# Overflow tiles of a top-6 mixture of experts on eight cores: taken out by GpSimd, found by halving a bit word, signalled by column halves

## The reference, cut to what matters

```python
probs = softmax(tokens @ router_w.T + router_b)
top_p, top_i = top_k(probs, 6)            # of 16 experts
gate[token, top_i] = top_p / sum(top_p)
out = sum over e of (x @ expert_w[e]) * gate[:, e]   # each 1024x1024
x = layernorm(x + out)
```

## Time and profile before

| | us |
|---|---|
| median of 3 runs | 1737.99 (1735.62 to 1738.44) |
| profiled execution, time | 1736.6 |
| its span, slowest core (0) | 1735.1 |
| its span, core with no overflow (5) | 1679.0 |
| TensorE busy | 1585.0 (91%) |
| ScalarE busy | 1307.4 (75%) |
| VectorE busy | 728.3 (42%) |
| GpSimd busy | 72.9 (4%) |

### The profile page before, as it was taken

The page is one execution under the profiler, slowest core; times in us unless marked ns, Lnnn a source line. Parts: engine busy times, 40 slices in busy tenths (PEclk is TensorE's granted clock), DMA queues, the critical chain, the costliest instruction groups (busy, mean ns, idle before and its releaser), DMA issues.

```text
span 1735.1 us, 55148 instructions; the slowest of 8 cores (1679.0 to 1735.1 us)
## 1 busy us (share of the span) xinstructions
PE 1585.0 (91%) x23176; PEld 987.5 (57%) x23176; DVE 728.3 (42%) x1722; ACT 1307.4 (75%) x1626; POOL 72.9 (4%) x55
## 2 busy tenths in 40 slices
PE   6999999999999999999977779999959999969996
PEld 3566556555665555655645445555636666636663
DVE  3132222222222222222227777666625666636587
ACT  2799999999999999999999866565525555525453
POOL 1000000000000000000000000000000000000056
PEclk9999999999999999999998889999979999989998
DMA  9920010010100100100050041026104133104012
GB/s 148 246 58 2 2 21 2 2 21 2 20 2 2 20 2 2 21 2 2 2 99 2 2 80 20 2 51 117 33 1 99 23 78 68 32 1 99 3 75 122
DMA packets 9877, 68.95 MB, mean 40 GB/s; under 512 B 1232, under 2 KB 1264, under 8 KB 6544
## 3 DMA queue, kind: packets, MB, share of 16 engines
q0 software_dynamic: 5008, 48.46, 15.6%
q1 hardware_dynamic: 4608, 16.78, 2.6%
HBM read 105.11 MB, written 8.39 MB: 65 GB/s over the span
## 4 chain that ended last, share of the span: by engine, by line
PE 81%; issue 6%; DVE 6%; ACT 3%; DVEq 2%; DMA 1%; ACTq 0%; POOL 0%; another core or an unknown queue 0%; PEldq 0%; POOLq 0%
PE s_PS L657 26%; PE s_PS L332 14%; PE s_PS L360 14%; PE s_PS L230 9%; PE s_PS L670 6%; PE s_PS L254 6%; PE s_PS L645 4%; ACT s_PR L341 3%; DVEq L171 2%; DMA s_XT<-xs 1%; DVE s_X1B L455 1%; DVE s_ST L408 1%; DVE s_KV L269 0%; DVE s_ACC L396 0%; PE s_PS L630 0%
## 5 line engine op out<-in xcount | busy, mean ns | idle before, releaser
L341 ACT ACTIVATE s_PR<-s_PS 128x1024 bf16<-128x1024 f32 x1024 | 947.9, 1204 | 42.5 <-PE s_PS L332 40.0
L332 PE MATMUL s_PS<-s_KV 64*128 64x256 bf16 x4096 | 352.8, 275 | 46.3 <-ACT s_PR L341 36.9
L729 ACT ACTIVATE s_PR<-s_PS,s_GS 128x512 bf16<-128x512 f32 x256 | 175.0, 686 | 260.4 <-PE s_PS L657 149.2
L360 PEld LDWEIGHTS s_PS<-s_KV,s_PR 128*128 128x128 bf16 x8192 | 285.0, 98 | 111.3 <-issue 111.3
L360 PE MATMUL s_PS<-s_KV,s_PR 128*128 128x65 bf16 x8192 | 347.0, 195 | 0.8 <-issue 0.8
L733 DVE SCALAR_TENSOR_TENSOR s_PR<-s_PS,s_GS,s_PR 128x512 bf16<-128x512 f32 x256 | 190.8, 749 | 228.5 <-ACT s_PR L729 220.4
L332 PEld LDWEIGHTS s_PS<-s_KV 64*128 64x128 bf16 x4096 | 142.5, 94 | 242.3 <-issue 197.1
L657 PE MATMUL s_PS<-s_KV,s_WP 128*64 128x512 bf16 x2080 | 241.2, 384 | 7.5 <-DVEq L852 3.0
L657 PE MATMUL s_PS<-s_XT,s_WP 128*64 128x512 bf16 x2080 | 242.2, 386 | 5.7 <-DVEq L852 3.0
L230 PE MATMUL s_PS<-s_XT,s_WP 128*128 128x512 bf16 x768 | 209.0, 382 | 21.4 <-DMA s_XT<-xs 15.1
L242 DVE CAST s_KV<-s_PS 128x512 bf16<-128x512 f32 x96 | 66.3, 691 | 336.6 <-PE s_PS L230 307.5
(11 more groups left out here) (93 smaller groups left out, 687.8 us busy)
## 6 DMA issues: line engine op xcount, KB each, us to landing
s_XT<-ew POOLq DMA_DIRECT2D x8, 2048.0 KB, 18.0
s_KV<-ew POOLq DMA_DIRECT2D x8, 2048.0 KB, 18.4
s_XT<-xs POOLq DMA_DIRECT2D x8, 1024.0 KB, 35.8
s_ACC<-xtm SPq DMA_DIRECT2D x16, 512.0 KB, 17.8
y<-s_ACC SPq DMA_DIRECT2D x16, 512.0 KB, 2.6
s_WP<-wp POOLq DMA_DIRECT2D x7, 768.0 KB, 7.0
s_WP<-wp POOLq DMA_DIRECT2D x1, 512.0 KB, 14.2
s_WP<-wp POOLq DMA_DIRECT2D x1, 256.0 KB, 5.8
```

What stands on the lines that cost most here:

```text
L332: return t.matmul(PS[:, o:o + 256], kt_buf(c)[rows, (kc + k) * 128:(kc + k + 1) * 128], q_buf(c)[rows, qb * 256:(qb + 1) * 256], start=Tru ...
L341: act[n] = S.tick(lambda s: s.activation(PR[:, (n % RING) * 1024:(n % RING + 1) * 1024], PS[:, i * 1024:(i + 1) * 1024], AF.Exp, bias=-3.0 ...
L360: return t.matmul(PS[:, o:o + 65], PR[:, p:p + 128], v_buf(c)[:, v0:v0 + 65], start=(kc + k == 0 and h == 0 and q == 0), stop=(kc + k == N ...
L729: hi_tok[(u, jh)] = S.tick(lambda s, h=h, b=b: s.activation(hi(u)[:, h], bank(b), AF.Copy, bias=0.0, scale=GS[:, u % 4:u % 4 + 1]))
```

## The change

1. GpSimd takes the overflow tile out (rows, gates, and the slot matrix as two comparisons of 64 columns instead of one of 128) and signals `oG`. It takes the next one when TensorE has signalled `oC`, behind the copy of the gathered tokens.
2. GpSimd and VectorE find the tile by halving: test the eight bits of each half of the word, then four, two, one. VectorE's body for a tile now begins with the wait for the gathered tokens. Its drain ahead of the search is gone.
3. TensorE gathers first and turns after. Its waits ahead of a spill, one for each token before, are now the highest value for each semaphore.
4. The two column halves of the product, of the scaling, of the low part and of the putting back are signalled one by one.
5. ScalarE copies the gathered tokens first and the turned matrix after. At the head of a round, before it waits, it does a copy of one element.
6. TensorE and ScalarE no longer wait at the end of a round for VectorE's additions. TensorE's wait for `oP` is at the head of a round. Behind each spill VectorE's list has a new drain with a signal (`added`), which joins the tokens of the two banks that the additions read.

```diff
-    many_reg, tile_reg = {}, []
+    V.do(lambda v: v.sem_inc(oP, 1))
+    V.do(lambda v: v.sem_inc(oA, 1))
+    many_reg, tile_reg = {}, {}
...
-        weights = [e_tok[2 * p], e_tok[2 * p + 1]]
-        banks_free = [tok for b in range(8) for tok in free[b]]
+        latest = {}
+        for sem, v in ([tok for b in range(8) for tok in free[b]] + [e_tok[2 * p], e_tok[2 * p + 1]]):
+            latest[id(sem)] = (sem, max(v, latest.get(id(sem), (sem, 0))[1]))
+        ready = list(latest.values())
...
-        for line in (T, V, S):
+        for line in (T, V, S, G):
             line.wait(flag_tok[0])
...
+        def tiles(e, work):
...
+            e.reg_load(word, FLG[0:1, NPE + p:NPE + p + 1])
+
+            def among(t0, t1):
+                e.reg_alu(part, word, (1 << t1) - (1 << t0), ALU.bitwise_and)
+                with e.If_ne(part, 0):
+                    if t1 - t0 == 1:
+                        work(e, t0)
+                    else:
+                        among(t0, (t0 + t1) // 2)
+                        among((t0 + t1) // 2, t1)
+
+            among(0, NT // 2)
+            among(NT // 2, NT)
...
+        def take_tile(e, t):
+            e.tensor_copy(OX, x1b(t))
+            e.tensor_copy(OG3, G3[:, (t * NE + 2 * p) * 3:(t * NE + 2 * p + 2) * 3])
+            for i in range(2):
+                col = t * NE + 2 * p + i
+                ins = e.tensor_scalar(OPUT[:, i * SLOTS:(i + 1) * SLOTS], CI[:, SLOTS:2 * SLOTS],
+                                      RK[:, col:col + 1], None, ALU.is_equal)
+            ins.then_inc(oG, 1)
+            e.wait_ge(oC, 1)
+            e.sem_clear(oC)
...
                 with e.Fori(0, n):
-                    e.wait_ge(oV, 1)
-                    for mm in turn_mms(OG3, OPUT) + gather_mms(OX, OPUT):
+                    e.wait_ge(oP, 1)
+                    e.sem_clear(oP)
+                    e.wait_ge(oG, 1)
+                    e.sem_clear(oG)
+                    for mm in gather_mms(OX, OPUT) + turn_mms(OG3, OPUT):
                         ins = mm(e)
                     ins.then_inc(oT, 1)
                     e.wait_ge(oS, 1)
-                    for mm in expert_mms(p, 0, YB[0], OXS) + expert_mms(p, 1, YB[1], OXS):
-                        ins = mm(e)
-                    ins.then_inc(oT, 1)
-                    e.wait_ge(oV, 3)
-                    for mm in back_mms(0, OPT, h0, l0) + back_mms(1, OPT, h0, l0):
-                        ins = mm(e)
-                    ins.then_inc(oT, 1)
-                    e.wait_ge(oV, 4)
+                    e.sem_inc(oC, 1)
+                    for jh in range(2):
+                        for mm in expert_mms(p, jh, YB[jh], OXS):
+                            ins = mm(e)
+                        ins.then_inc(oT, 1)
+                    for jh in range(2):
+                        e.wait_ge(oV, 2 + jh)
+                        for mm in back_mms(jh, OPT, h0, l0):
+                            ins = mm(e)
+                        ins.then_inc(oT, 1)
                     e.sem_inc(oE, 1)
-                    e.wait_ge(oP, 1)
-                    e.sem_clear(oP)
...
         def one_tile(e, t):
-            e.tensor_copy(OX, x1b(t))
-            e.tensor_copy(OG3, G3[:, (t * NE + 2 * p) * 3:(t * NE + 2 * p + 2) * 3])
-            put_op(e, OPUT, RK[:, t * NE + 2 * p: t * NE + 2 * p + 2], SLOTS).then_inc(oV, 1)
             e.wait_ge(oS, 1)
             e.reduce_sum(OGS[:, :], PS[:, MB * 512 + 128: MB * 512 + 131],
                          axis=AX.X).then_inc(oV, 1)
-            e.wait_ge(oS, 2)
             for jh in range(2):
+                e.wait_ge(oS, 2 + jh)
                 h = slice(jh * 512, (jh + 1) * 512)
-                ins = e.scalar_tensor_tensor(l0[:, h], bank(YB[jh]), OGS[:, :], h0[:, h],
-                                             ALU.mult, ALU.subtract)
-            ins.then_inc(oV, 1)
-            e.wait_ge(oT, 3)
+                e.scalar_tensor_tensor(l0[:, h], bank(YB[jh]), OGS[:, :], h0[:, h],
+                                       ALU.mult, ALU.subtract).then_inc(oV, 1)
             for jh in range(2):
+                e.wait_ge(oT, 4 + jh)
                 a = acc(t, jh * 512, (jh + 1) * 512)
-                ins = e.tensor_tensor(a, bank(OB2[jh]), a, ALU.add)
-            ins.then_inc(oV, 1)
+                e.tensor_tensor(a, bank(OB2[jh]), a, ALU.add)
+            e.drain()
             e.wait_ge(oE, 2)
...
                 with e.Fori(0, n):
-                    e.wait_ge(oT, 1)
-                    e.activation(OPT, bank(MB, 128), AF.Copy, bias=0.0, scale=1.0)
-                    e.activation(OXS, PS[:, GB * 512: GB * 512 + 1024], AF.Copy, bias=0.0,
-                                 scale=1.0).then_inc(oS, 1)
-                    e.wait_ge(oT, 2)
-                    e.wait_ge(oV, 2)
...
-                    e.wait_ge(oV, 4)
-                    e.sem_inc(oE, 1)
+                    e.activation(LG[0:1, 0:1], EX[0:1, 0:1], AF.Copy, bias=0.0, scale=1.0)
                     e.wait_ge(oA, 1)
                     e.sem_clear(oA)
+                    e.wait_ge(oT, 1)
+                    e.activation(OXS, PS[:, GB * 512: GB * 512 + 1024], AF.Copy, bias=0.0, scale=1.0)
+                    e.activation(OPT, bank(MB, 128), AF.Copy, bias=0.0, scale=1.0).then_inc(oS, 1)
+                    e.wait_ge(oV, 1)
+                    for jh in range(2):
+                        e.wait_ge(oT, 2 + jh)
+                        h = slice(jh * 512, (jh + 1) * 512)
+                        e.activation(h0[:, h], bank(YB[jh]), AF.Copy, bias=0.0,
+                                     scale=OGS[:, :]).then_inc(oS, 1)
+                    e.sem_inc(oE, 1)
...
+        added = V.tick(lambda v: v.drain())
+        for b in OB2:
+            free[b] = free[b] + [added]
```

More of the change, by code:

```diff
@@ L775, in flags @@
         flag_tok.append(V.tick(lambda v: v.tensor_copy(FLG[:, :], EX[0:1, 0:2 * NPE])))
-    oT, oV, oS, oE, oP, oA = (mksem(n) for n in ("oT", "oV", "oS", "oE", "oP", "oA"))
-    many_reg, tile_reg = {}, []
+    oT, oV, oS, oG, oC, oE, oP, oA = (
+        mksem(n) for n in ("oT", "oV", "oS", "oG", "oC", "oE", "oP", "oA"))
+    V.do(lambda v: v.sem_inc(oP, 1))
+    V.do(lambda v: v.sem_inc(oA, 1))
+    many_reg, tile_reg = {}, {}
     def spill(p, u):
         h0, l0 = hi(u + 1), lo(u + 1)
-        weights = [e_tok[2 * p], e_tok[2 * p + 1]]
-        banks_free = [tok for b in range(8) for tok in free[b]]
+        latest = {}
+        for sem, v in ([tok for b in range(8) for tok in free[b]] + [e_tok[2 * p], e_tok[2 * p + 1]]):
+            latest[id(sem)] = (sem, max(v, latest.get(id(sem), (sem, 0))[1]))
+        ready = list(latest.values())
         back = sc_tok[(u - 1, 1)]
-        for line in (T, V, S):
+        for line in (T, V, S, G):
             line.wait(flag_tok[0])
@@ L794, in many, with gpsimd @@
             return many_reg[id(e)]
+        def tiles(e, work):
+            if id(e) not in tile_reg:
+                k = len(tile_reg)
+                tile_reg[id(e)] = (e.alloc_register(f"tiles{k}"), e.alloc_register(f"tile{k}"))
+            word, part = tile_reg[id(e)]
+            e.reg_load(word, FLG[0:1, NPE + p:NPE + p + 1])
[9 more added lines that the diff above has]
+            among(NT // 2, NT)
+        def gpsimd(e):
+            n = many(e)
+            with e.If_ne(n, 0):
+                tiles(e, take_tile)
+        def take_tile(e, t):
[8 more added lines that the diff above has]
+            e.sem_clear(oC)
         def tensor(e):
@@ L798, in tensor @@
             with e.If_ne(n, 0):
-                for sem, v in banks_free + weights:
+                for sem, v in ready:
                     e.wait_ge(sem, v)
                 with e.Fori(0, n):
-                    e.wait_ge(oV, 1)
-                    for mm in turn_mms(OG3, OPUT) + gather_mms(OX, OPUT):
+                    e.wait_ge(oP, 1)
[3 more added lines that the diff above has]
+                    for mm in gather_mms(OX, OPUT) + turn_mms(OG3, OPUT):
                         ins = mm(e)
@@ L821, in vector @@
             with e.If_ne(n, 0):
-                e.drain()
-                if not tile_reg:
-                    tile_reg.extend([e.alloc_register("tiles"), e.alloc_register("tile")])
-                e.reg_load(tile_reg[0], FLG[0:1, NPE + p:NPE + p + 1])
-                for t in range(NT):
-                    e.reg_alu(tile_reg[1], tile_reg[0], 1 << t, ALU.bitwise_and)
-                    with e.If_ne(tile_reg[1], 0):
-                        one_tile(e, t)
+                tiles(e, one_tile)
         def one_tile(e, t):
-            e.tensor_copy(OX, x1b(t))
-            e.tensor_copy(OG3, G3[:, (t * NE + 2 * p) * 3:(t * NE + 2 * p + 2) * 3])
-            put_op(e, OPUT, RK[:, t * NE + 2 * p: t * NE + 2 * p + 2], SLOTS).then_inc(oV, 1)
             e.wait_ge(oS, 1)
@@ L859, in scalar @@
                 with e.Fori(0, n):
-                    e.wait_ge(oT, 1)
```

(16 more changed lines are left out.)

## The result

The changed kernel takes 0.9885 of the time before (interval 0.9866 to 0.9904), that is about 1718 us against a median of 1738.22 for the kernel before beside it; measured again the ratio is 0.9874 (0.9858 to 0.9889). Its four runs gave 1718.75, 1716.91, 1800.35 and 1836.83 us; in the last two the cores of one die ran at a granted clock of 0.87 to 0.93, so the ratio leaves them out. The profiled execution is the one of 1718.75. So the direction was right, the gain is 20 us where 30 were forecast, and the time lies about 2 us above the top of the range.

A forecast was written before the change was run, and what follows sets the result against it. It took the slowest core to be bound by TensorE plus two spills: 1681.6 us without them plus 2 x 12.4 gave a span of 1706.4, and with 1.5 above the span 1707.9, say 1707.5; range 1702 to 1716.

The forecast's parts named there:

- The base: Span of the slowest core without its spills, taken from core 4 as 1681.6 us.
- The bank wait of 1.7: Ahead of a spill, TensorE waits 1.7 us until VectorE's additions free the last bank.
- ScalarE's 1.4: Between gather and product, ScalarE's copies with hand-overs take 1.4 us, the table load hidden under the wait.
- the second half's tail of 1.6: Behind the product, only one half's scaling, low part and hand-overs remain: 1.6 us.
- The head of the round: Some eight waits and clears on TensorE as a spill begins: 0.5 us, between 0.14 and 0.78.
- Gather and turn: TensorE's gather and turning matmuls in a spill: 0.5 us, or 1.1 at the low clock.
- The product: The spill's product on TensorE: 4.9 us, the middle between 3.5 at full clock and 6.2 at the low one.
- Ends of pairs without overflow: New token and GpSimd's test at all seven pair ends cost TensorE 0, at most 0.2 us each.
- Behind the spill, 0.8 us: TensorE's next unit after a spill loses 0.8 us to slow clock or VectorE's remaining work, between 0 and 2.5.
- slower: the ends of empty pairs: Rival: late `added` costs TensorE 0 to 1.2 us at seven pair ends, 1716 us at 1.2; chance 0.03.
- The clock stays low: Rival: TensorE's clock stays low through the whole spill, 3.9 us more each, 1715 us; chance 0.13.
- VectorE's search is late: Rival: all eight search tests are long, VectorE ready 4.8 us late per spill, 1717 us; chance 0.08.

The follow-up runs named there:

- e1: Changed kernel without VectorE's drain and token behind each spill; TensorE waits for oP from the spill's body instead: 0.983 of the kernel before, two-spill mean 659.2 us against 665.3.
- e4: Changed kernel with 12 unread filler matmuls ahead of the gather and 6 ahead of the product: 0.9854 of the kernel before, two-spill mean 661.5 us.
- e2: Changed kernel with TensorE's bank wait split, the gather waiting only for banks that gather and product write: 0.9836 of the kernel before, two-spill mean 660.5 us.
- e8: Changed kernel with VectorE's body written once in a loop over tiles, only the two additions unrolled: 0.9831 of the kernel before, two-spill mean 661.0 us.

## Why the prediction was right and wrong

**Right.** The base: core 0 without its spills comes to 1682.6 us here (first gather at 1020.6, 634.4 of core 5, and 27.7 from the last gather to the end), 1.0 above the 1681.6 used. GpSimd has the tile in time: its copy begins at 1211.0, 64 us ahead of TensorE's stop, and takes 1040 ns, not 2.0:

```profile
L828 POOL COPY s_WP<-s_XT x2: 1036/1040/1044, 1211.0 to 1451.6; 128x1024 bf16<-128x1024 bf16 x2
```

The bank wait of 1.7, ScalarE's 1.4 (measured 1.5), the second half's tail of 1.6 (1.8), the putting back of 0.5 (0.6), the way out of 0.5 (0.2) and the hidden table load held. So did the direction, and the clock that falls and comes back during the product. Not so core 2: it did not come out below all cores with two spills (1708.7 against 1708.3 of core 1).

**Off in size, inside the spill: 2.0 us each.** The head of the round took 1.19 (1276.70 to 1277.89) where 0.5 was put: I knew two bounds, 0.14 and 0.78, from steps with one wait, and the head has several one behind the other. Gather and turn took 1.20, the term for the low clock, where 0.5 was taken because TensorE was to be idle for only 2.2 us; it was idle for 2.89. The product took 5.26 for 4.9. I had expected the clock to be up through the product in some spills; the trace shows 5.0 to 6.4 from the product's start to the putting back for all twelve tiles. The two spills of core 0 come to 13.5 and 13.7 for 11.6 each; the forecast was 4.0 too little.

**The step that failed: "Ends of pairs without overflow ... I take 0, at the most 0.2 each", and with it "Behind the spill, 0.8 us".** Both rest on VectorE's long step of 1.1 to 1.2. Core 0 pays 34.5 - 27.2 = 7.3 us outside its two spills, where 1.6 was forecast. The waits of TensorE on core 0 in the expert part:

```profile
PE s_PS L670 <- DVEq L912: 6.7, 4, 2.7
```

Counted by how late each unit starts behind the one before, against the same place on core 5, the 7.3 are 2.2 behind the second spill, 1.2 and 1.1 at two pairs without overflow, 2.1 at the last pair, where core 5 waits too but less, and 0.7 scattered. The argument from the earlier trace rows, that the old jump had ended by 1382.36, looked at when VectorE had to be back, not at how long its jump was, and left out that a drain behind the jump is now awaited by TensorE. "Behind the spill" had VectorE done 4 to 5 us after the putting back; behind core 0's second spill it took 6.2 (1537.31 to the drain at 1543.51), 3.09 of them one jump. Measured from test to drain, the way over sixteen bodies is 2.7 to 3.2 us at 48 of 53 places and 4.2 to 4.3 at the other five, two of them core 0's.

The rival "slower: the ends of empty pairs" had the right place and mechanism; its size was about 1 us at two of core 0's pairs and 2 at the last, far from the 4.9 for each that it needed to turn the sign.

The kernel before had the same long jump, and its trace shows it. This is core 5, without a tile, at its last two pairs, in the chain in order of time; L821 is the test for no overflow, L793 the first record of the next pair's code:

```profile
1582.70 0.06 DVEq L821
...
1586.41 0.31 DVEq L793
...
1586.75 0.06 DVEq L821
...
1589.93 0.02 DVEq L61
```

From test to next record are 3.7 and 3.2 us. At the first of these places the eight cores show 3.4 to 3.8; at the second, the five cores without a spill there show 3.1 to 3.5, and ScalarE's scaling, which VectorE needs next, had ended about 1.5 us or more before VectorE came back. So it was the jump that took the time. At nearly all other pair ends of before, among them, the next record is a wait that ends with ScalarE's scaling, and only tells that the jump took no more than 3.4 to 4.2 us. Where it can be seen the jump was no shorter before the change; what the change added is a drain behind it for which TensorE waits.

e1 is the proof: with the drain gone, core 0 got 10.8 us back, of which 7.7 lie at these four places, 1.7 in two shorter spills, and 1.4 are spread over the rest.

**Two rivals came true in part.** "The clock stays low": the gather ran at the low clock as the rival says, the put-back (0.62) and the next unit (3.64) did not, and the product was low for 3.3 of its 5.3 us. Against a product at full clock e4 puts the price at 1.6 on core 0; the rival has 2.7 and the forecast's own term 1.4. "VectorE's search is late": not on core 0, where VectorE waits for ScalarE, but on cores 1 and 6, which did not set the time. Core 1:

```profile
1605.57 5.00 PE L657 MATMUL s_PS<-s_KV,s_WP 128*64 128x512 bf16 x32 [1.56 <-ACT s_PR L899]
...
1609.73 0.16 DVE L871 TENSOR_REDUCE s_OGS<-s_PS 128x1 f32<-128x3 f32 x1 [9.82 <-issue]
```

The slow clock hides most of it: with a product of 3.64 such a search sets the spill's length, as e4 showed, and in e2 the put-back on core 1 came 9.5 us behind the product's start.

**The account.** 1.0 base, 4.0 inside the spills and 5.7 outside are the 10.7 us by which 1717.1 stands above the forecast span of 1706.4. The three terms are differences within one trace, so that they add up is no test of their causes; the causes rest on e1 for the part outside and on e4 for the clock. The head of the round is read off the trace; no experiment shortened it (in e2, where no bank is waited for, it still takes 1.25). The largest error is the jump, whose one long row of 1.23 in the earlier trace rows was taken for the size of all.

## What to carry to other kernels

A token that is raised behind a data-dependent search, and awaited by the engine that sets the time, makes the whole search part of the path, on the cores that have nothing to search for as well: raise it inside the body that did the work, and wait for it only where that body ran. When a step leaves the critical path, price what stands behind it at its own longest row, not at the row that was on the path, and look for that row on a core where nothing else hides it; here core 5 of the kernel before had it, 3.2 to 3.7 us. Splitting a chain of steps over four engines into column halves was worth 6.8 us by the two-spill mean, moving the search to an idle engine 5.5; by the ratios, 0.9912 and 0.9919, the two can't be put in order. Both were worth more than a cleverer search (nothing).

## What the runs showed of the hardware

**One and the same jump takes half a microsecond or three.** VectorE's way over sixteen bodies took 2.7 to 3.2 us at 48 of 53 places and 4.2 to 4.3 at five; with the code made small (e8) it took 0.5 to 0.6 at 35 of 53 places and still 2.7 or more at 13. In the kernel before it took 3.1 to 3.8 where it can be seen. The Trainium skill (Runtime: NRT & Kernel Launch, "Instruction fetch mechanics") says that a taken branch out of the loaded blocks waits for the fetch. The fall with smaller code fits that; no trace shows what was loaded.

**The clock of a short piece of work behind idle time.** With idle times of 2.0 to 4.6 us ahead of the gather and 1.6 to 1.7 ahead of the product, the product took 4.9 to 6.6 us for all twelve tiles of the kernel after; at a granted clock of 1.00 it takes 3.64. On core 0 the clock was still 1.00 for the first 1.7 us of idle time, 0.50 in the gather and 1.00 again behind 3.3 us of the product. With 1.25 and 1.55 of idle time (e2) the product came out at 3.64 or at 6.55 on the same core in the same kernel. Eighteen filler matmuls (e4) brought it to 3.64 for all twelve tiles.

**Waits on several semaphores add up.** Between the last bank's release and the first gather matmul there are 1.19 us with nothing but waits, clears and a loop's head: four waits for banks, two register moves and two pairs of wait and clear, whose records on TensorE's sequencer start 0.1 us apart, once 0.2, with no bank left to wait for.

**GpSimd against VectorE is not one ratio.** The copy of 128x1024 in bf16 takes 1.04 us on GpSimd and 0.43 on VectorE, 2.4 times; the operation in the earlier trace rows 4.65 times. The Trainium skill (GPSIMD Engine Reference, "Engine selection") has one input near line rate. The copy's 1.04 us are 1.0 ns for each element of a partition, the operation's 3.78 us 3.7 ns; as a ratio to VectorE neither is near one.
